# First attention of a vision tower: scores in row tiles of 32, two parts of six heads, 17 value columns, another order on all engines

## What is computed

```python
xh = x.reshape(b, n, h, hd)                       # x = layernorm(tokens)
qkv = jnp.einsum('bnhd,hde->bnhe', xh, W_qkv) + b_qkv
q, k, v = jnp.split(qkv, 3, axis=-1)
scores = jnp.einsum('bihd,bjhd->bhij', q, k) / f ** 0.5
p = jax.nn.softmax(scores, axis=-1)
attn = jnp.einsum('bhij,bjhd->bihd', p, v)
out = attn.reshape(b, n, f) @ W_out + b_out        # added to the tokens
```

## Time and profile before

| | us |
|---|---|
| median of three runs | 1250.88 (1250.23 to 1251.78) |
| the profiled execution | 1248.16 |
| its span, first to last instruction | 1246.2 |
| tokenizer, to 98.66 | 98.7 |
| attention B, 98.66 to 298.11 | 199.5 |
| the rest | 948.1 |

### The profile page before, as it was taken

The page is one execution under the profiler, slowest core; times in us unless marked ns, Lnnn a source line. Parts: engine busy times, 40 slices in busy tenths (PEclk is TensorE's granted clock), DMA queues, the critical chain, the costliest instruction groups (busy, mean ns, idle before and its releaser), DMA issues.

```text
span 1246.2 us, 26649 instructions
## 1 busy us (share of the span) xinstructions
PE 1157.0 (93%) x8874; PEld 1006.4 (81%) x8874; DVE 929.7 (75%) x2392; ACT 863.4 (69%) x3158; POOL 451.8 (36%) x477
## 2 busy tenths in 40 slices
...
## 3 DMA queue, kind: packets, MB, share of 16 engines
...
## 4 chain that ended last, share of the span: by engine, by line
PE 63%; DVE 18%; ACT 13%; issue 4%; POOL 1%; DMA 0%; SPq 0%; DVEq 0%; POOLq 0%; ACTq 0%
ACT t_p L1219 7%; PE bank L1478 6%; PE bank L379 5%; PE bank L1452 4%; DVE f_eq L1873 4%; PE bank L1402 3%; PE bank L1469 3%; PE bank L1443 3%; PE bank L1422 3%; PE bank L1406 2%; PE bank L1403 2%; PE bank L1405 2%; PE bank L1404 2%; PE bank L1431 2%; PE bank L1978 2%
## 5 line engine op out<-in xcount | busy, mean ns | idle before, releaser
L1219 ACT ACTIVATE t_p<-bank,t_nmax 108x108 f32<-108x108 f32 x792 | 270.5, 368 | 33.8 <-DVE t_nmax L763 32.5
L1063 POOL TENSOR_TENSOR t_sq<-t_raw 108x768 f32<-108x768 f32 x88 | 154.3, 1754 | 138.7 <-ACT t_raw L1169 137.8
L2107 POOL TENSOR_TENSOR f_hid_lo<-f_hid,f_hid_hi 128x432 fp32r<-128x432 f32 (+2 forms) x144 | 143.6, 1017 | 107.2 <-ACT f_hid_hi L2093 106.8
L1219 ACT ACTIVATION_READ_ACCUMULATOR t_p<-bank,t_nmax 108x1 f32 x792 | 175.3, 221 | 0.0
L763 DVE TENSOR_REDUCE t_nmax<-bank 108x2 f32<-108x216 f32 (+1 forms) x242 | 121.9, 519 | 41.9 <-PE bank L1443 25.2
L2093 ACT CAST f_hid_hi<-f_hid 128x432 fp32r<-128x432 f32 (+2 forms) x144 | 72.4, 515 | 115.2 <-DVE f_hid L2064 92.1
L780 DVE TENSOR_TENSOR t_p<-t_p,t_rinv 108x432 f32<-108x432 f32 x198 | 142.4, 719 | 6.8
L1452 PE MATMUL bank<-ident,t_p 108*108 108x108 f32 x792 | 110.4, 262 | 22.9 <-ACT t_pT L1227 21.0
L1452 PEld LDWEIGHTS bank<-ident,t_p 108*108 108x108 f32 x792 | 82.0, 133 | 55.7 <-ACT t_pT L1227 34.9
L1227 ACT COPY t_pT<-bank 108x432 f32<-108x432 f32 x198 | 106.7, 539 | 26.8 <-PE bank L1452 26.7
L2064 DVE SCALAR_TENSOR_TENSOR f_hid<-bank,f_maskT 128x432 f32<-128x432 f32 (+2 forms) x77 | 39.6, 514 | 97.8 <-PE bank L1939 93.5
...
## 6 DMA issues: line engine op xcount, KB each, us to landing
...
```

Of the source, the lines that this page charges most:

```text
L1063: pool.tensor_tensor(sq, v, v, ALU.mult).then_inc(s["sq"], 1)
L1219: act.activation(b.p[g % 2][:, m, :], self.scores_of(g, m), ACT.Exp, bias=b.nmax[:, m:m + 1], accum_out=b.rsum[:, m:m + 1]).then_inc(s["ex ...
L2107: pool.tensor_tensor(self.hid_lo[m % 4][:, c], self.hid[m % 4][:, c], self.hid_hi[m % 4][:, c].bitcast(F32), ALU.subtract).then_inc(s["lo" ...
```

## The change

Keys are no longer spread. The scores of a part are six matmuls over 32 rows: part c takes heads 2c and 2c+1 of each of the three tiles, the two heads of a tile on neighbouring row tiles and in different banks. There are two parts of six heads, each of which fills both banks; a part waits for all exponentials of the part before it. The probabilities lie in another order of heads (`kept`). The row maxima are taken in four pieces of three heads, reciprocals and products in two of six. V is projected and copied with 17 columns a head; the rest of the V buffers is set to zero once. VectorE copies X (from group 3 on) and Q out of PSUM, ScalarE copies K. On all three engines the order within a group is written anew. In the weight preparation, two one-row casts on ScalarE and a fill on GpSimd give way to one copy of 33 rows on GpSimd. The input `row_of` and its transfer go, and the constants' wait counts 64 for 80. The order of `turns` follows that of TensorE.

```diff
-        if g == 8:
-            act.wait_ge(s_centred, 3)
-            act.wait_ge(s_zero, 2)
-            act.copy(splitC[3][64:65, :], rawb[64:65, :]).then_inc(s_hi, 1)
-        if g == 9:
-            act.copy(splitC[3][96:97, :], rawb[96:97, :]).then_inc(s_hi, 1)
...
-        pool.memset(splitC[3][64:97, :].bitcast(F32), 0.0).then_inc(s_zero, 1)
...
-        pool.wait_ge(s_hi, 4)
+
+        pool.wait_ge(s_centred, 3)
         pool.wait_ge(s_lo, 2)
+        pool.tensor_copy(splitC[3][64:97, :], rawb[64:97, :]).then_inc(s_bias, 1)
+        pool.wait_ge(s_bias, 1)
         pool.tensor_tensor(splitC[3][96:97, :], rawb[96:97, :], splitC[3][96:97, :].bitcast(F32),
                            ALU.subtract).then_inc(s_lo, 1)
...
+        self.v_used = 17
...
-        self.inits = 7 if small else 12
-
-
-        self.s_parts = 3 if small else 2
-        self.max_parts = 3 if small else 4
+        self.inits = 11 if small else 12
+
+
+
+        self.s_parts = 2
+        self.max_parts = 4
+        self.pn_parts = 2 if small else 3
...
+            return turn[0] == "qk" and turn[2] == 1 or turn[0] == "x" and turn[1] >= 3
+        return turn[0] == "qk" and kind == "D" and turn[2] >= 2
...
+    def kept(self, hd):
+
+        return hd % 4 * self.tiles + hd // 4
...
+                halves = [(self.sbank[0], 6 * c, 3), (self.sbank[1], 6 * c + 3, 3)]
...
-            sl = slice(4 * c, 4 * c + 4)
-            after(dve, s["exp"], nth(g, 12, 4 * c + 3))
+            n = HEADS // self.pn_parts
+            sl = slice(n * c, n * c + n)
...
-        def spread_k(g):
-            after(dve, s["T"], self.turned("qk", g, 0))
+        def copy_x(g):
+            after(dve, s["T"], self.turned("x", g))
+            dve.tensor_copy(b.xt[g % 3][:, 0:3, :],
+                            self.turn_bank("x", g)[:, 0:3 * GT].rearrange("p (a n) -> p a n", a=3)).then_inc(s["kev"], 1)
+
+        def copy_q(g):
+            after(dve, s["T"], self.turned("qk", g, 1))
             after(dve, s["S"], self.scored(g - 2))
-            src = self.turn_bank("qk", g, 0)[:, 0:3 * GT].rearrange("p (t n) -> p t n", t=3)
-            shape = [128, 3, 4, GT]
-            dve.tensor_tensor(b.kS[g % 2][:, :, :].rearrange("p (t j) n -> p t j n", j=4),
-                              src.unsqueeze(2).to_broadcast(shape),
-                              self.row_of[:, :].unsqueeze(1).unsqueeze(3).to_broadcast(shape),
-                              ALU.mult).then_inc(s["kev"], 1)
+            dve.tensor_copy(b.qT[g % 2][:, 0:3, :],
+                            self.turn_bank("qk", g, 1)[:, 0:3 * GT].rearrange("p (a n) -> p a n", a=3))\
+               .then_inc(s["kev"], 1)
...
-            dve.tensor_copy(b.v[g % 4][:, 0:384], self.qbank[0][0:GT, 0:384])\
+            dve.tensor_copy(b.v[g % 4][:, 0:384].rearrange("p (a d) -> p a d", d=32)[:, :, 0:self.v_used],
+                            self.qbank[0][0:GT, 0:HEADS * self.v_used].rearrange("p (a d) -> p a d", d=self.v_used))\
...
+            for k in range(4):
+                dve.memset(b.v[k][:, 0:384], 0.0).then_inc(s["init"], 1)
...
             if this:
                 row_max(g, 0)
             if before:
-                weigh(g - 1, 2)
-            if g + 1 < GROUPS:
-                spread_k(g + 1)
+                weigh(g - 1, 1)
+            if g + 3 < GROUPS:
+                copy_x(g + 3)
             if g + 4 < GROUPS:
                 norm_apply(g + 4)
+            if g + 6 < GROUPS:
+                norm_stats(g + 6)
             if this:
                 row_max(g, 1)
+            if g + 1 < GROUPS:
+                copy_q(g + 1)
+            if this:
                 weigh(g, 0)
-            if g + 6 < GROUPS:
-                norm_stats(g + 6)
             if g >= 2:
                 residual(g - 2)
-            if this:
-                row_max(g, 2)
-                weigh(g, 1)
...
+            if kind == "B":
+                for n in range(6):
+                    if n % 3 == 0:
+                        after(act, s["max"], nth(g, 4, 2 * c + n // 3))
+                    m = 6 * c + n
+                    act.activation(b.p[g % 2][:, m, :], self.sbank[n // 3][0:GT, n % 3 * GT:(n % 3 + 1) * GT], ACT.Exp,
+                                   bias=b.nmax[:, m:m + 1], accum_out=b.rsum[:, m:m + 1]).then_inc(s["exp"], 1)
+                return
...
         yield
         for g in range(GROUPS + 2) if kind == "B" else ():
             this, before = g < GROUPS, 0 < g <= GROUPS
-            if this:
-                exps(g, 0)
             if g >= 2:
-                copy_o(g - 2, 0)
-            if before:
-                copy_p(g - 1, 0)
-            if g + 3 < GROUPS:
-                copy_x(g + 3)
-            if this:
-                exps(g, 1)
-            if before:
-                copy_p(g - 1, 1)
-            if g + 1 < GROUPS:
-                copy_qk(g + 1, 1)
+                copy_p(g - 2, 1)
+                copy_p(g - 2, 2)
             if g and g + 5 < GROUPS:
                 norm_root(g + 5)
             if this:
-                exps(g, 2)
+                exps(g, 0)
+            if g + 1 < GROUPS:
+                copy_qk(g + 1, 0)
             if before:
-                copy_p(g - 1, 2)
+                copy_p(g - 1, 0)
+            if g >= 2:
+                copy_o(g - 2, 0)
+            if this:
+                exps(g, 1)
             if beside:
                 beside(act, g)
...
-                    mm = pe.matmul(dst[0:GT, 128 * t:128 * t + 128], b.xt[g % 3][:, t, :], self.w[:, t, 2, :],
+                    n = 4 * self.v_used
+                    mm = pe.matmul(dst[0:GT, n * t:n * t + n], b.xt[g % 3][:, t, :],
+                                   self.w[:, t, 2, :].rearrange("p (a d) -> p a d", d=32)[:, :, 0:self.v_used],
...
-                after(pe, s["exp"], nth(g, 12, 4 * c - 1) - 4)
-                pe.matmul(self.sbank[(3 * g + c) % 2][0:GT, 0:4 * GT], b.qT[g % 2][:, c, :],
-                          b.kS[g % 2][:, 4 * c:4 * c + 4, :], start=True, stop=True).then_inc(s["S"], 1)
+                after(pe, s["exp"], 12 * g + 6 * c)
+                for t in range(self.tiles):
+                    for j in range(2):
+                        lo, hi = self.head_rows(2 * c + j)
+                        mm = pe.matmul(self.sbank[j][0:GT, t * GT:(t + 1) * GT], b.qT[g % 2][lo:hi, t, :],
+                                       b.kS[g % 2][lo:hi, t, :], start=True, stop=True)
+                mm.then_inc(s["S"], 1)
...
-            after(pe, s["pn"], nth(g, 3, c))
+            after(pe, s["pn"], nth(g, self.pn_parts, (4 * c + 3) * self.pn_parts // HEADS))
...
-                                   b.pT[:, hd, :], start=True, stop=True)
+                                   b.pT[:, self.kept(hd) if kind == "B" else hd, :], start=True, stop=True)
...
                 turn_qk(g + 1, 0)
+            if g >= 2:
+                values(g - 2, 0)
             if before:
                 turn_p(g - 1, 0)
-            if g >= 2:
-                values(g - 2, 0)
             if g + 3 < GROUPS:
                 turn_x(g + 3)
             if this:
                 scores(g, 1)
+            if g + 1 < GROUPS:
+                turn_qk(g + 1, 1)
             if before:
                 turn_p(g - 1, 1)
             if g >= 2:
                 output(g - 2)
-            if g + 1 < GROUPS:
-                turn_qk(g + 1, 1)
-            if this:
-                scores(g, 2)
             if before:
                 turn_p(g - 1, 2)
             if g + 2 < GROUPS:
```

51 lines of the change are left out of this document (24 added, 27 removed).

## The result

The changed kernel takes 1265.51 us in the median (1260.53 to 1272.01), the kernel before 1250.96 beside it; the ratio is 1.0119, with a 95% interval from 1.0069 to 1.0170. The profiled execution took 1272.01, the longest of its four, so the traces stand 23.7 us apart (spans 1269.9 and 1246.2) where the medians stand 14.6 apart. That may be part of this spread; it isn't shown for these four executions.

The account below looks back on a forecast made before the run. It took three engines as about equally full, with TensorE pacing an undisturbed group. 99.1 + 21 x 7.2 + 24.4 + 15.7 = 290.4 for 298.1, 7.7 us less: 1243.2 by the median, range 1231 to 1254.

Parts of the forecast that it names:

- the period: Time of one undisturbed group of three images in the first attention: 7.2 us for 7.60, bounds 7.04 and 7.6.
- the disturbance: Time that the next stage's weight preparation costs beside the first attention's groups: 24 us, between 13 and 34, for 23 before.
- the start: Before group 0's first scores: Q is copied by VectorE after the tokenizer's last step, 0.4 us later.
- GpSimd's new pair: Copy of 33 rows, then the third subtraction, after group 7: one or two VectorE products held, 3.5 us, from 0 to 9.
- Scores, spread keys, maxima: Scores of 12 records last 0.82 us; VectorE loses 1.50 of key spreading a group; four maxima of 0.49, slot 0.41.
- rival A: Scores on TensorE: 32-row matmuls of a pair don't overlap, 0.57 more a part, 24 us, 1267, slower; chance 7%.
- 17 value columns: V projection on TensorE moves 68 columns for 128: 0.43 us for 0.65; the V copy falls to some 0.31.
- Tile shape: Change of tiling mode on TensorE, four a group: about 0.1 us in part 1; another 0.15 a drain would cost 6 in all.
- The ring: Scores, first maximum, six exponentials, then the next part's scores, which wait for them: 3.52 us a part, 7.04 a group.
- rival B: No change: the ring's tight places each lose a bit and the period stays 7.6; 1251.5, 1249 to 1253; chance 11%.
- The means: VectorE's means and subtractions come after the V copy, next scores' reduction about 1.35 us late; four groups, 5.4.
- Rival C: GpSimd's long stretch blocks products in every part of it and in groups 15 and 16: 1254, slower; chance 9%.

Follow-up runs that it names:

- run without reads: Changed kernel without the accumulator reads behind the first attention's exponentials, so probabilities aren't normalised: period 7.02, median 1257.06 us, ratio 1.0051 to the kernel before.
- run with unread matmuls: Changed kernel with matmuls that nothing reads in TensorE's idle time, before group 0 and in groups 0 to 5: 1259.64 us, ratio 1.0075.
- the means moved: Changed kernel with VectorE's six means and subtractions ahead of the residual and V copy instead of behind them: 1258.63 us, ratio 1.0057.
- the three edits together: Changed kernel with GpSimd's five subtractions in six pieces each, VectorE's means moved ahead, and unread matmuls in TensorE's idle time: 1237.26 us, ratio 0.9897.
- the changed kernel in pieces: Changed kernel with GpSimd's subtractions, VectorE's means and subtractions and ScalarE's casts cut small, plus unread matmuls at the start: 1229.12 us, ratio 0.9828.
- the two quiet kernels: Kernel before and changed kernel, means and subtractions on the first head only, casts moved behind the last group: stages 176.1 and 181.8 us.
- the two kernels in pieces: Changed kernel, and old attention with new preparation (no unread matmuls), each with all work beside the groups cut small: 1229.12 and 1237.13 us.

## Why the prediction was wrong

The forecast was 7.7 us less; the trace has 23.7 more. From the first scores to the end of the stage it had 191.3 and there are 218.5: 7.8 from the period, 19.1 from the disturbance, 0.3 from the tail. The disturbance is what the groups take above 7.57 each, 43.5 us for the forecast's 24.3 (the sum has 24.4; its terms add up to 24.3): the start 7.0 for nothing, the four periods with VectorE's beside work alone 11.6 for 5.4, periods 6 and 8 with GpSimd's new pair 17.8 for 13.2, periods 16 and 17 7.5 for 3.7. The 2 us set aside for the clock lie within these, and the last period is 0.2 short.

**Scores, spread keys, maxima: right.** 12 records last 0.82 as forecast, two maxima 0.90, the product 0.83, the X and Q copies 0.49. The rows of 64-row pairs carried over the earlier trace rows, and rival A is out.

**17 value columns: mis-sized.** The slot of 0.43 was made by taking the columns in proportion. It is 0.63, of which 0.04 is the change of tile shape (0.59 ahead of 128-row scores); 60 columns save 0.12 a group by the run with 32 value columns. Little of a small matmul's slot is its columns; what the rest is, the runs don't separate.

**Tile shape: right.** 0.1 was taken in part 1, and 0.12 is there (0.75 for 0.67 on Q, 0.63 for 0.59 on V). The further 0.15 a change that I named as a possible price isn't. Part 1 is 3.85 for 3.70, by the V projection.

**The ring: 3.71 for 3.52.** Six exponentials were right (2.11 for 2.08). The first begins 0.59 behind the maximum for 0.53, and the scores 0.15 behind the last read for 0.05: both handovers were put at the smallest that the rows showed. Together with part 1 that makes 7.57 for 7.2, 7.8 us in 21 groups, and is rival B's period. The forecast's shape was right: ScalarE sets one half and TensorE the other, and the run without reads gained in the one half alone.

**The start: the step that was missing.** I gave it 0.4 us ahead of the first scores and nothing behind them. Groups 0 to 2 take 8.0 more than before in the trace. I took the granted clock as a small loss behind stalls (2 us in all), from a mean of 0.85 over one bad stretch, and read no stretch of the old start for what keeps the clock there. In the new kernel the same 1.2 GHz that the old one leaves by group 1 (0.61 granted from 98.66 to 103, 1.00 from 103 to 106) lasts up to 26 us. Why is left open; by the runs it is neither idle time alone nor sure to be cured by filling it.

**The means: 2.84 for 1.35.** The direct lateness was 1.17 (run with unread matmuls), near the forecast. The rest is the slow clock that the wait of 1.74 calls forth, 1.67 a group, which no forecast by durations alone contains.

**GpSimd: the place was wrong.** The prediction said that a product of VectorE would stand behind GpSimd's subtraction in groups 5 and 7, for 3.0. What stands is VectorE's own subtraction of the means, longer by 4.6 and 4.5, since the cast that starts GpSimd and VectorE's beside work come at the same point of the group; with the clock behind it periods 6 and 8 are 8.8 and 9.0 over, where the forecast had 4.8 for stall and cast together. This instruction too has two operands in SBUF. The Trainium skill, SBUF — State Buffer, section Who interferes with whom, says of any VectorE instruction with two SBUF inputs that it contends with a GpSimd instruction that reads SBUF; the trace agrees for both instructions, and the prediction had applied the rule to the product alone. For the casts of groups 15 and 16 (periods 16 and 17) the prediction said "nothing, but by 0.2 only; 3 us each if it slips": it slipped, the products begin 0.18 and 0.66 behind GpSimd and stand 4.8 and 4.3 us. A margin smaller than the error of the sum was taken as safe. Rival C, with a chance of 9%, had these two products right, and the sign of the whole. Its long stretch was not where the time went (the next paragraph), and its 1254 is 11 short.

**The new GpSimd copy: right in this trace.** The pair of copy and subtraction holds two products, 1.68 and 2.00 for 0.83, 2.0 in all, within the 0 to 9 and near the 3.5; with the means moved the same subtraction held one for 5.24, so the price is one of meeting. That the copy, which reads SBUF, holds the product until it ends is as the same section of the Trainium skill has it. Groups 9 to 11, where the one-row casts and a held product had lain, take 5.7 us less, the one place in the stage where the changed kernel clearly gains. The old attention with the new preparation gained only 1.2 there: periods 10 and 11 fell by 3.3, and period 9 rose by 2.05, where GpSimd's pair now met a product.

**Behind the stage.** 3.4 us of the traces' difference lie some 600 to 780 us behind the stage, in work that is the same in both kernels, where two clock patterns occur: 948 us in the traces of the kernel before, the three edits together, the changed kernel in pieces and the new preparation, 951.5 to 955 in the other ten (the two quiet kernels, whose casts lie there, not counted). The stretch from 600 to 700 us behind the stage is granted 0.90 in the four and 0.85 in the other kernels. I can't put it down to the change; it may be how an execution falls. The rest of the whole's difference between the two kernels in pieces is of this kind, so of their 8 us only 2, in one trace of each, can be put to the attention.
